# A transformer block for eight sequences: an earlier start of batch 0, one tile earlier for batch 3, and q's rows stored ahead of k's reading

## The chip, the cores and the metric

The kernel runs on one core of a Trainium2 chip. The metric is the device time of one execution in microseconds, the median of several runs. A profile is one such execution, taken with the hardware profiler.

## The reference, cut to what matters

The input is eight sequences of 512 tokens with 256 features. Each goes through three steps, and each step adds to the sequence:

```python
x = x + 0.5 * ffn(layernorm(x))        # ffn: fft, times a sparse 256x256 complex matrix, real part of ifft, + bias
x = x + attention(layernorm(x))        # q, k, v from the left 128 features; 16 heads of 8; softmax; Wo; + bo
x = x + 0.5 * ffn(layernorm(x))
```

The ffn is linear, so the kernel folds it at its start into one real matrix of 256x256, `half_ffn`, that already holds the factor 0.5. The mean and the variance of the layernorm are taken beside the product: x1 = (product of the raw rows) * rstd + x + half of the bias.

## The kernel before, in words

Five engines run side by side, each with an instruction list of its own that is carried out strictly in its written order: TensorE (`pe`, the matmuls), ScalarE (`act`, above all the exponentials), VectorE (`dve`, everything that leaves PSUM), GpSimd (`pool`, the reciprocal roots and the additions of biases) and SyncE (`sp`, the transfers). Semaphores are the only link: an engine that waits holds all that stands behind it in its list.

The work for one batch is cut into 16 quads of four heads by 128 keys. For a quad TensorE makes the scores (`score_products`, L799), ScalarE the exponentials (L669, two instructions of 128x1024), and TensorE multiplies them with the values (`value_quad`, L828) into the bank `ot`. The outer loop (`it`, L908 and on) goes over the batches, and the inner one over 16 slots `s`. In a slot TensorE issues the scores of the next quad, then the jobs of the slot, then the products of this quad with the values.

The jobs are the rest of the work: `F1_t` (first ffn of tile t), `LT`/`KT`/`QT`/`V` (normed left half transposed, keys, queries, values), `N` (norms for the guard), `WO_t` (output product) and `F2_t` (second ffn). Which job runs in which slot for which batch is written in tables at the file's head: `BEGIN` for iteration 0, `FIRST` for iteration 1, `STEADY`, `LATE` and `END` for the others. An entry `("F1_1", 2, LEFT)` in iteration 1 works for batch 3. All jobs share the bank `misc`; a job waits on TensorE until VectorE has evacuated all jobs of earlier slots.

Two helpers on VectorE matter here. `left_half(b)` (L957) subtracts the mean and multiplies with the reciprocal root; it waits for `rstd_done[1]`, which GpSimd raises in `rstd_of(1, ...)` (L548 and L550). `turn_left(b)` (L966) transposes the result into `left_blocks`; SyncE stores that to `left_scr` and loads it back as `leftT`, from which `KT_0` is made in slot 14. The calls in the loop over slots are

```python
if s == (8 if it else 10):
    left_half(it + 2, range(0, 2))
if s == (9 if it else 10):
    left_half(it + 2, range(2, T))
    if it:
        turn_left(it + 2)
```

GpSimd's list for iteration `it` is `end_of(it - 1)` (L563, L553 for x_out), `rstd_of(2, it)`, which waits for the moments of x2 that VectorE makes at the end of slot 5 (L946), `begin_x2(it)` (two additions of 128x512, L563 and L553), and only then `rstd_of(1, it + 3)`.

The keys and queries of a batch are spread over the partitions by way of memory: `k_out` stores `kp` to `k_scr` (L393), `k_in` loads it back as `KS` in two transfers (L400), `q_out` and `q_in` do the same with `qp`, `q_scr` and `QS` (L396, L404). SyncE issues all of them.

A guard (`guard`, L833) decides for each batch whether the scores are so large that an exact branch has to compute the attention. TensorE loads the flag from memory into a register and branches. With these inputs the branch isn't taken.

Before the loops lies an opening (`PROLOGUE`): the folding of the ffn, F1 of batches 0 and 1, LT, KT, QT, V and N of batch 0, and the first two score quads.

## Time and profile before

| what | value |
|---|---|
| median of three runs | 315.89 us (313.49 to 320.12) |
| the profiled execution's own time | 312.38 us |
| its span | 310.5 us |
| TensorE busy in the span | 294.8 us (95%) |
| ScalarE busy | 257.6 us (83%) |
| VectorE busy | 190.5 us (61%) |
| GpSimd busy | 98.3 us (32%) |
| TensorE's granted clock | full in every slice |

The span goes from the first to the last instruction; 1.9 us of the execution's own time lie outside of it. Times in the rows below count from the start of the span. PE is the matmuls of TensorE and PEld its weight loads, DVE is VectorE, ACT is ScalarE, POOL is GpSimd, SPq is what SyncE issues. In a row of the timeline the first number is the start, the second the time until the end of the last instruction of the row, then the engine, the line, the operation, what it writes and reads, the number of instructions, and in brackets how long the engine had been idle before it and what ended that.

### The profile page before, as it was taken

Reading aid. Unit: us, or ns where it says so; the run is one execution under the profiler, and the core shown is the slowest. Engines: PE = TensorE matmul, PEld = TensorE weight load, DVE = VectorE, ACT = ScalarE, POOL = GpSimd, SP = SyncE. Lnnn points to the kernel's source line nnn. Section 1 sums busy time; section 2 is a strip of 40 time slices with the busy share of each in tenths; the row PEclk is TensorE's granted clock in tenths of the full one; section 3 lists DMA queues with packets and bytes.
Section 4 is the critical chain, followed back from the end, with each engine's and each line's share of the span. In section 5 each row is a group of like instructions: output and inputs, shape, how many; then the busy total and the mean of one; then the engine's idle time right before and its main releaser. Section 6 shows DMA issues by size and latency. Waiting matters only on the chain.

```text
span 310.5 us, 8810 instructions
## 1 busy us (share of the span) xinstructions
PE 294.8 (95%) x3440; PEld 112.5 (36%) x3443; DVE 190.5 (61%) x552; ACT 257.6 (83%) x285; POOL 98.3 (32%) x113
## 2 busy tenths in 40 slices
PE   8887999899998999999999999999999999998996
PEld 5633333233332333333333333334333333322333
DVE  1688546747775678657776678567755643370255
ACT  2117998898997889998998989998999999999921
POOL 6562531223604053223604251313600340034005
PEclk9999999999999999999999999999999999999999
DMA  7935615573462762665453663554372464112102
GB/s 192 337 137 192 218 65 153 195 270 133 139 217 83 245 208 103 208 204 217 155 192 129 231 205 112 198 172 143 131 238 104 138 205 170 38 68 70 37 34 70
DMA packets 25891, 49.33 MB, mean 159 GB/s; under 512 B 2032, under 2 KB 14192, under 8 KB 24048
## 3 DMA queue, kind: packets, MB, share of 16 engines
q1 hardware_dynamic: 25152, 48.26, 46.0%
q10 hardware_dynamic: 688, 0.40, 0.8%
q8 instruction: 32, 0.52, 0.7%
q14 instruction: 19, 0.16, 0.2%
HBM read 31.08 MB, written 17.56 MB: 157 GB/s over the span
## 4 chain that ended last, share of the span: by engine, by line
PE 75%; DMA 9%; DVE 5%; ACT 5%; issue 3%; POOL 3%; SPq 0%; ACTq 0%; POOLq 0%
PE ot L828 28%; PE misc L719 26%; PE scores L799 15%; ACT probs L669 5%; DMA leftT<-left_scr 4%; DMA q_scr<-qp 2%; PE scores L719 2%; DMA QS<-q_scr 2%; DMA left_scr<-left_blocks 1%; POOL x L553 1%; PE scores L686 1%; PE scores L693 1%; DVE left_blocks L966 1%; DVE lh L957 1%; POOL rstd L550 1%
## 5 line engine op out<-in xcount | busy, mean ns | idle before, releaser
L669 ACT ACTIVATE probs<-scores 128x1024 f32<-128x1024 f32 x256 | 243.8, 1028 | 20.6 <-PE scores L799 20.3
L828 PE MATMUL ot<-probs,VS 128*32 128x512 f32 x1024 | 133.9, 594 | 2.9 <-ACT probs L669 2.3
L799 PE MATMUL scores<-QS,KS 32*128 32x512 f32 x512 | 64.7, 495 | 3.0 <-DMA QS<-q_scr 1.3
L799 PEld LDWEIGHTS scores<-QS,KS 32*128 32x128 f32 x512 | 24.5, 181 | 109.8 <-ACT probs L669 101.0
L828 PEld LDWEIGHTS ot<-probs,VS 128*32 128x32 f32 x1024 | 30.6, 109 | 25.8 <-ACT probs L669 5.0
L563 POOL TENSOR_TENSOR x_out<-x,half_bias 128x512 f32<-128x512 f32 x7 | 9.0, 1292 | 88.8 <-DVE x L1012 88.8
L548 POOL TENSOR_SCALAR veps<-mv 128x4 f32<-128x4 f32 (+1 forms) x25 | 6.1, 242 | 95.9 <-DVE mv L946 95.9
L1017 DVE SCALAR_TENSOR_TENSOR x_out<-misc,rstd,x_out 128x256 f32<-128x256 f32 x28 | 13.5, 484 | 33.7 <-PE misc L719 30.2
L719 PE MATMUL misc<-half_ffn,xT 128*32 128x256 f32 x448 | 32.1, 386 | 0.0
L719 PE MATMUL misc<-half_ffn,xT_in 128*32 128x256 f32 x400 | 27.1, 385 | 1.4 <-DVE half_ffn L1193 1.3
L550 POOL TENSOR_TENSOR rstd<-veps,power 128x4 f32<-128x4 f32 (+1 forms) x25 | 25.3, 1013 | 2.1
L939 DVE BATCH_NORM_STATS2 stats<-x 128x6 f32<-128x256 f32 x64 | 23.2, 411 | 0.0
L1012 DVE TENSOR_TENSOR x<-misc,x 128x256 f32<-128x256 f32 x30 | 11.3, 419 | 16.7 <-PE misc L719 16.7
L993 DVE SCALAR_TENSOR_TENSOR x<-misc,rstd,x_in 128x256 f32<-128x256 f32 x24 | 11.6, 484 | 14.8 <-PE misc L719 14.8
L553 POOL TENSOR_TENSOR x_out<-x,half_bias 128x512 f32<-128x512 f32 x9 | 11.5, 1285 | 19.7 <-DVE x L1012 19.7
L1056 DVE STREAM_TRANSPOSE ot_t<-ot 128x512 f32<-128x512 f32 x16 | 11.5, 716 | 8.8 <-PE ot L828 8.8
L719 PE MATMUL misc<-wo_sb,otn 128*32 128x256 f32 x240 | 16.1, 385 | 0.6 <-DVE otn L1070 0.6
L972 DVE STREAM_TRANSPOSE x_blocks<-x 128x512 f32<-128x512 f32 x14 | 16.3, 1165 | 0.5
L719 PEld LDWEIGHTS misc<-half_ffn,xT 128*32 128x32 f32 x448 | 10.9, 108 | 11.7 <-issue 5.6
L719 PEld LDWEIGHTS misc<-half_ffn,xT_in 128*32 128x32 f32 x400 | 10.4, 109 | 11.8 <-issue 5.1
L983 DVE CAST kp<-misc 128x256 fp32r<-128x256 f32 x14 | 5.9, 424 | 13.8 <-PE misc L719 12.5
L939 DVE BATCH_NORM_STATS2 stats<-x_in 128x6 f32<-128x256 f32 x32 | 11.6, 410 | 0.0
(125 smaller groups left out, 260.0 us busy)
## 6 DMA issues: line engine op xcount, KB each, us to landing
KS<-k_scr SPq DMA_DIRECT2D x14, 512.0 KB, 4.9
QS<-q_scr SPq DMA_DIRECT2D x14, 512.0 KB, 4.6
x_in<-x SPq DMA_DIRECT2D x8, 512.0 KB, 5.1
xT_in<-x_t SPq DMA_DIRECT2D x8, 512.0 KB, 6.4
k_scr<-kp SPq DMA_DIRECT2D x8, 512.0 KB, 3.0
q_scr<-qp SPq DMA_DIRECT2D x8, 512.0 KB, 4.4
x_scr<-x_blocks SPq DMA_DIRECT2D x7, 512.0 KB, 2.9
xT<-x_scr SPq DMA_DIRECT2D x7, 512.0 KB, 4.7
```

Of the source, the lines that this page charges most:

```text
L550: nc.gpsimd.tensor_tensor(to[:, tiles], veps[k][:, tiles], power[:, tiles], ALU.pow).then_inc(rstd_done[k], 1)
L553: nc.gpsimd.tensor_tensor(dst[:, tiles, :], src[:, tiles, :], row[:, :].unsqueeze(1).to_broadcast([P, tiles.stop - tiles.start, E]), ALU.a ...
L669: nc.scalar.activation(probs[u % PRING][:, :, :], scores[u % SRING][:, :, :], ACT.Exp, scale=SCORE_SCALE).then_inc(exp_done, 1)
L719: last = mm(dst[COL * j:COL * (j + 1), :], weights(j), rhs, start=c == 0, stop=c == len(terms) - 1)
L799: last = mm(scores[(u + j // 2) % SRING][:, j % 2, :], KS[b % 2][rows, slot, kt * P:(kt + 1) * P].bitcast(F32R), QS[b % 2][rows, slot, :]. ...
L828: last = mm(ot[COL * j:COL * (j + 1), :], VS[b % 2][:, kt, h, :], probs[(u + j // 2) % PRING][:, j % 2, :], start=s % 8 == 0, stop=s % 8 == 7)
L939: ins = nc.vector.bn_stats(stats[k][:, t, :], src[:, t, :])
L972: last = nc.vector.transpose(x2_blocks[:, :, 2 * i:2 * i + 2, :], x2[:, 2 * i:2 * i + 2, :].rearrange("p t (f k) -> p k t f", k=E // 32))
L993: return nc.vector.scalar_tensor_tensor(x1[b % 3][:, i, :], tile, rstd[0][b % 2][:, i:i + 1], biased[:, i, :], ALU.mult, ALU.add)
L1012: nc.vector.tensor_tensor(x2[:, i, :], tile, x2[:, i, :], ALU.add).then_inc(evacuated, 1)
L1017: nc.vector.scalar_tensor_tensor(x_out[:, i, :], tile, rstd[2][0][:, i:i + 1], x_out[:, i, :], ALU.mult, ALU.add).then_inc(evacuated, 1)
L1056: nc.vector.transpose(ot_t[:, :, :].rearrange("p c r -> p (c r)"), ot[:, :]).then_inc(ot_taken, 1)
```

## The change

- **Opening.** `half_bias` is made between ScalarE's four copies and not behind them. GpSimd adds it to tiles 0 and 1 of batch 0 ahead of its first reciprocal root. VectorE makes the statistics of x1 of batch 0 for tiles 0 and 1 as soon as they are there, GpSimd takes their roots apart from those of tiles 2 and 3, and two of the four statistics of batch 1's input are made first. The evacuation of F1_3 of batch 1 is moved behind those of KT and QT.
- **Values of batch 0's first quad.** `value_products(0, 0)` is issued ahead of the guard's branch, and once more inside of the branch, which isn't taken.
- **Iteration 1.** F1_1, F1_2 and F1_3 of batch 3 move from slots 4, 5 and 6 to slots 1, 4 and 5; slot 6 is empty. `left_half` of batch 3 moves from slots 8 and 9 to 7 and 8, with `turn_left` in slot 8.
- **Transfers.** `q_out(1)` stands ahead of `k_in(1)`.

On TensorE, around the first guard. Before (the register load of L835 follows the second score quad at once):

```order
L799 MATMUL scores<-QS,KS 128x512 x4
L788 MATMUL misc<-kp,pick 128x512 x2
L788 MATMUL ot<-qp,pick 128x512 x2
L799 MATMUL scores<-QS,KS 128x512 x4
L835 TENSOR_LOAD safe
L835 ISA x2
L836 COMPARE_AND_BRANCH
```

and with the change, where `ot<-probs,VS` is the first value product:

```order
L810 MATMUL scores<-QS,KS 128x512 x4
L799 MATMUL misc<-kp,pick 128x512 x2
L799 MATMUL ot<-qp,pick 128x512 x2
L810 MATMUL scores<-QS,KS 128x512 x4
L844 MATMUL ot<-probs,VS 32x512 x4
L851 TENSOR_LOAD safe
L851 ISA x2
L852 COMPARE_AND_BRANCH
```

The four value matmuls now stand ahead of the load of the flag.

On VectorE, slots 5 to 9 of iteration 1 (`x_0<-misc` is x1 of batch 3, `x` the x2 of batch 0, `lh` the normed left half, `VS` the values). Before:

```order
L946 BN_AGGR mv<-stats 128x2 x4
L993 SCALAR_TENSOR_TENSOR x_0<-misc,rstd_1,x_in 128x256
L939 BN_STATS stats<-x_0 128x6 x2
L946 BN_AGGR mv<-stats 128x2 x4
L983 CAST qp<-misc 128x256
L985 TENSOR_TENSOR qp<-misc,qp 128x256
L1056 STREAM_TRANSPOSE ot_t<-ot 128x512
L983 CAST qp<-misc 128x256
L985 TENSOR_TENSOR qp<-misc,qp 128x256
L957 TENSOR_SCALAR lh<-x_0,mv,rstd_0 128x128 x2
L1030 COPY VS<-misc 128x16x8 x4
L957 TENSOR_SCALAR lh<-x_0,mv,rstd_0 128x128 x2
```

and with the change:

```order
L966 BN_AGGR mv<-stats 128x2 x4
L959 BN_STATS stats<-x 128x6 x2
L966 BN_AGGR mv<-stats 128x2 x4
L1004 CAST qp<-misc 128x256
L1006 TENSOR_TENSOR qp<-misc,qp 128x256
L1077 STREAM_TRANSPOSE ot_t<-ot 128x512
L978 TENSOR_SCALAR lh<-x_0,mv,rstd_0 128x128 x2
L1004 CAST qp<-misc 128x256
L1006 TENSOR_TENSOR qp<-misc,qp 128x256
L978 TENSOR_SCALAR lh<-x_0,mv,rstd_0 128x128 x2
L987 STREAM_TRANSPOSE left_blocks<-lh 128x512
L1051 COPY VS<-misc 128x16x8 x4
```

The first half of `lh` stands ahead of the second evacuation of q, and `left_blocks` ahead of the values; the moments of x2 are the second of the two groups of `mv` and no longer the first.

On SyncE, the rows of batch 1. Before:

```order
L393 DMA k_scr<-kp 128x2x512
L400 DMA KS<-k_scr 64x1x2048 x2
L396 DMA q_scr<-qp 128x2x512
L404 DMA QS<-q_scr 64x1x2048 x2
L393 DMA k_scr<-kp 128x2x512
```

and with the change:

```order
L399 DMA k_scr<-kp 128x2x512
L402 DMA q_scr<-qp 128x2x512
L406 DMA KS<-k_scr 64x1x2048 x2
L410 DMA QS<-q_scr 64x1x2048 x2
L399 DMA k_scr<-kp 128x2x512
```

The store of q is issued ahead of the two loads of k.

```diff
@@ -74,7 +74,8 @@
           12: [("F2_1a", -1, LEFT), ("F2_1", -1, LEFT)], 13: [("F2_2a", -1, LEFT), ("F2_2", -1, LEFT)],
           14: [("KT_0", 2, RIGHT)], 15: [("KT_1", 2, RIGHT)]}
 
-FIRST = {**STEADY, 0: [("F1_0a", 2, LEFT), ("F1_0", 2, LEFT)], 1: []}
+FIRST = {**STEADY, 0: [("F1_0a", 2, LEFT), ("F1_0", 2, LEFT)], 1: [("F1_1a", 2, LEFT), ("F1_1", 2, LEFT)],
+         4: [("F1_2a", 2, LEFT), ("F1_2", 2, LEFT)], 5: [("F1_3a", 2, LEFT), ("F1_3", 2, LEFT)], 6: []}
 
 BEGIN = {3: [("LT", 1, LEFT)], 4: [("KT_0", 1, RIGHT), ("F1_0a", 2, LEFT)], 5: [("F1_0", 2, LEFT), ("QT_0", 1, RIGHT)],
          6: [("KT_1", 1, RIGHT), ("F1_1a", 2, LEFT)], 7: [("F1_1", 2, LEFT), ("QT_1", 1, RIGHT)],
@@ -103,7 +104,7 @@
     if it == PROLOGUE:
 
         ahead = [(f"F1_{t}", 2) for t in range(T)]
-        jobs = [(f"F1_{t}", 1) for t in range(T)] + [("LT", 1)] + ahead + [("KT", 1), ("QT", 1), ("N", 1)]
+        jobs = [(f"F1_{t}", 1) for t in range(T)] + [("LT", 1)] + ahead[:-1] + [("KT", 1), ("QT", 1), ahead[-1], ("N", 1)]
         return {s: [(name, d, LEFT)] for s, (name, d) in enumerate(jobs)}
     if it == EPILOGUE:
 
@@ -319,6 +320,11 @@
         mv_done = [sem(f"mv_done{i}") for i in range(3)]
         veps_done = [sem(f"veps_done{i}") for i in range(3)]
         rstd_done = [sem(f"rstd_done{i}") for i in range(3)]
+        ahead_biased = sem("ahead_biased")
+        first_stats = sem("first_stats")
+        first_mv = sem("first_mv")
+        first_veps = sem("first_veps")
+        first_rstd = sem("first_rstd")
         normed = sem("normed")
         ahead_ready = sem("ahead_ready")
         left_turned = sem("left_turned")
@@ -500,8 +506,8 @@
 
             load_x(3)
             k_out(1)
+            q_out(1)
             k_in(1)
-            q_out(1)
             q_in(1)
             for it in range(1, B):
                 if it + 1 < B:
@@ -581,15 +587,20 @@
                 rstd_of(0, b + 1)
                 add_rows(x_in[b % 2], x_in[b % 2], half_bias, xb_done)
 
-            rstd_of(0, 1)
             pool.wait_ge(bias_set, 1)
             pool.wait_ge(x_loaded[0], 16)
             add_row(x1[0], x_in[0], half_bias, early_biased, slice(0, 1))
             add_row(x1[0], x_in[0], half_bias, early_biased, slice(1, 2))
+            rstd_of(0, 1)
             add_row(x1[0], x_in[0], half_bias, xb_done, slice(2, T))
             pool.wait_ge(x_loaded[1], 16)
-            add_rows(x1[1], x_in[1], half_bias, xb_done)
-            rstd_of(1, 1)
+            add_row(x1[1], x_in[1], half_bias, ahead_biased, slice(0, 2))
+            pool.wait_ge(first_mv, 1)
+            nc.gpsimd.tensor_scalar(veps[1][:, 0:2], mv[1][:, 0:2, 1], EPS, None, ALU.add).then_inc(first_veps, 1)
+            pool.wait_ge(first_veps, 1)
+            nc.gpsimd.tensor_tensor(rstd[1][0][:, 0:2], veps[1][:, 0:2], power[:, 0:2], ALU.pow).then_inc(first_rstd, 1)
+            rstd_of(1, 1, slice(2, T))
+            add_row(x1[1], x_in[1], half_bias, xb_done, slice(2, T))
             rstd_of(0, 2)
             square(kp, sq_k, kp_step, 0)
             square(qp, sq_q, qp_step, 0)
@@ -629,12 +640,12 @@
             for piece, bank, copy in ((1, scores[0][:, 0], even[0]), (3, scores[1][:, 0], even[1])):
                 act.wait_ge(ffn_mm, piece)
                 nc.scalar.copy(copy[:, :, :], half_bank(bank)).then_inc(ffn_copied, 1)
+            act.wait_ge(bias_loaded, 16)
+            nc.scalar.mul(half_bias[:, :], bias_raw[:, :], 0.5).then_inc(bias_set, 1)
             for piece, bank, copy in ((5, scores[0][:, 0], even[2]), (6, scores[0][:, 1], odd)):
                 act.wait_ge(ffn_mm, piece)
                 nc.scalar.mul(copy[:, :, :], half_bank(bank), 0.5 / E).then_inc(ffn_copied, 1)
 
-            act.wait_ge(bias_loaded, 16)
-            nc.scalar.mul(half_bias[:, :], bias_raw[:, :], 0.5).then_inc(bias_set, 1)
             act.wait_ge(pick_loaded, 16)
             nc.scalar.copy(pick[:, :, :, :, :].rearrange("p n s i r -> p (n s i r)").bitcast(F32R),
                            pick_raw[:, :, :, :, :].rearrange("p n s i r -> p (n s i r)")).then_inc(pick_set, 1)
@@ -824,10 +835,15 @@
                 if s % 8 == 0:
                     wait(pe, ot_taken, 2 * b + g)
                 pe.wait_ge(exp_done, u + 2)
+                value_products(b, s).then_inc(quad_done, 1)
+
+            def value_products(b, s):
+                _, _, kt, heads = quad_units(s)
+                u = PAIRS * b + 2 * s
                 for j, h in enumerate(heads):
                     last = mm(ot[COL * j:COL * (j + 1), :], VS[b % 2][:, kt, h, :],
                               probs[(u + j // 2) % PRING][:, j % 2, :], start=s % 8 == 0, stop=s % 8 == 7)
-                last.then_inc(quad_done, 1)
+                return last
 
             def guard(b, taken):
 
@@ -864,6 +880,8 @@
                         pe.wait_ge(exact_taken, done + 1)
                         mm(misc[:, 0:E], attnT[:, :], wo_sb[:, :], start=True, stop=True).then_inc(exact_ready, 1)
                     pe.wait_ge(guarded, b + 1)
+                    if b == 0:
+                        value_products(0, 0)
                 with pe.Else():
                     pe.sem_inc(exact_ready, EXACT_MM)
 
@@ -901,6 +919,7 @@
             pe.wait_ge(evacuated, evac_count("N", 0))
             first_rows(3)
             score_quad(0, 1)
+            value_quad(0, 0)
             guard(0, evac_count("N", 0))
             pe.wait_ge(late_loaded, 32)
 
@@ -915,7 +934,8 @@
                     if it == 0 and 0 < s < 3:
                         keep_awake(1, misc[:, :])
                     run_jobs(it, s)
-                    value_quad(it, s)
+                    if it or s:
+                        value_quad(it, s)
                     if s == guard_slot(it) and it + 1 < B:
                         guard(it + 1, count_of_slots_to(it, s))
 
@@ -952,7 +972,8 @@
                     norm_stats(0, x_in[b % 2], t, t == T - 1)
 
             def left_half(b, tiles=range(T)):
-                dve.wait_ge(rstd_done[1], b + 1)
+                if b or tiles[-1] == T - 1:
+                    dve.wait_ge(rstd_done[1], b + 1)
                 for t in tiles:
                     last = nc.vector.tensor_scalar(lh[:, t, :], x1[b % 3][:, t, 0:HD], mv[1][:, t, 0:1],
                                                    rstd[1][0][:, t:t + 1], ALU.subtract, ALU.mult)
@@ -1202,20 +1223,41 @@
             norm0_stats(0)
             norm_moments(0, 1)
             fold(half_ffn, even[2], odd[:, :, :], ALU.subtract, ALU.add, 6, 4)
-            for s in range(T):
-                run_jobs(PROLOGUE, s)
-            norm0_stats(1)
-            left_half(0)
+            dve.wait_ge(mv_done[0], 1)
+            norm0_stats(1, range(0, 2))
+
+            def first_x1(t):
+                dve.wait_ge(evacuated, evac_count(f"F1_{t}", 0))
+                return nc.vector.bn_stats(stats[1][:, t, :], x1[0][:, t, :])
+
+            evacuate("F1_0", 0)
+            evacuate("F1_1", 0)
+            first_x1(0)
+            evacuate("F1_2", 0)
+            first_x1(1).then_inc(first_stats, 1)
+            dve.wait_ge(first_stats, 1)
+            for t in range(2):
+                last = nc.vector.bn_aggr(mv[1][:, t, :], stats[1][:, t, :])
+            last.then_inc(first_mv, 1)
+            evacuate("F1_3", 0)
+            first_x1(2)
+            first_x1(3).then_inc(stats_done[1], 1)
+            norm_moments(1, 1, range(2, T))
+            dve.wait_ge(first_rstd, 1)
+            left_half(0, range(0, 2))
+            norm0_stats(1, range(2, T))
+            left_half(0, range(2, T))
             norm_moments(0, 2)
 
-            run_jobs(PROLOGUE, T)
-            for t in range(T):
+            evacuate("LT", 0)
+            for t in range(T - 1):
                 evacuate(f"F1_{t}", 1)
-            run_jobs(PROLOGUE, 2 * T + 1)
-            run_jobs(PROLOGUE, 2 * T + 2)
+            evacuate("KT", 0)
+            evacuate("QT", 0)
+            evacuate(f"F1_{T - 1}", 1)
             dve.wait_ge(row_ready, 1)
             nc.vector.tensor_copy(KS[0][:, 0, :].bitcast(F32R), row_banks[0]).then_inc(first_k_set, 1)
-            run_jobs(PROLOGUE, 2 * T + 3)
+            evacuate("N", 0)
             for n, rows in ((2, KS[0][:, 1, :]), (3, QS[0][:, 1, :])):
                 dve.wait_ge(row_ready, n + 1)
                 nc.vector.tensor_copy(rows.bitcast(F32R), row_banks[n]).then_inc(second_set, 1)
@@ -1248,9 +1290,9 @@
                                 norm_stats(2, x2, t, t == T - 1)
                             norm_moments(2, it)
                     if it + 2 < B:
-                        if s == (8 if it else 10):
+                        if s == (10 if not it else 7 if it == 1 else 8):
                             left_half(it + 2, range(0, 2))
-                        if s == (9 if it else 10):
+                        if s == (10 if not it else 8 if it == 1 else 9):
                             left_half(it + 2, range(2, T))
                             if it:
                                 turn_left(it + 2)
```

## Rows read from the trace of the kernel before

**Rows 1.** The page: the chain that ended last, by engine.

```profile
PE 75%; DMA 9%; DVE 5%; ACT 5%; issue 3%; POOL 3%; SPq 0%; ACTq 0%; POOLq 0%
```

**Rows 2.** The waits of PE over the span: us in total, times, longest.

```profile
PE misc L719 <- DMA leftT<-left_scr: 1.8, 2, 1.5
```

**Rows 3.** Timeline of the opening, 12 to 21 us.

```profile
12.64 2.66 POOL L553 TENSOR_TENSOR x<-x_in,half_bias 128x256 f32<-128x256 f32 x3
...
13.47 0.48 DVE L993 SCALAR_TENSOR_TENSOR x<-misc,rstd,x 128x256 f32<-128x256 f32 x1 [1.70 <-POOL x L553]
...
19.17 1.12 DVE L957 TENSOR_SCALAR lh<-x,mv,rstd 128x128 f32<-128x128 f32 x4 [0.20 <-POOL rstd L550]
...
20.40 0.42 PEld L753 LDWEIGHTS misc<-ident,lh 128*128 128x128 f32 x4 [1.42 <-issue]
```

**Rows 4.** The instructions of GpSimd that write rstd, over the whole span.

```profile
L550 POOL TENSOR_TENSOR rstd<-veps,power x25: 715/1038/1052, 11.6 to 306.3; 128x4 f32<-128x4 f32 x23, 128x2 f32<-128x2 f32 x2
```

**Rows 5.** Timeline around the first guard, 29 to 32 us.

```profile
29.95 0.19 PEld L828 LDWEIGHTS ot<-probs,VS 128*32 128x32 f32 x8 [1.31 <-issue]
...
30.98 0.19 PEld L799 LDWEIGHTS scores<-QS,KS 32*128 32x128 f32 x4 [0.84 <-ACT probs L669]
...
31.54 7.51 ACT L669 ACTIVATE probs<-scores 128x1024 f32<-128x1024 f32 x8 [0.39 <-PE scores L799]
```

**Rows 6.** Timeline, the rows of k and q of batch 1, 46 to 63 us.

```profile
46.03 0.42 DVE L985 TENSOR_TENSOR qp<-misc,qp 128x256 fp32r<-128x256 f32 x1
...
48.80 1.16 SPq L400 DMA_DIRECT2D KS<-k_scr  x2
...
50.00 0.59 SPq L396 DMA_DIRECT2D q_scr<-qp  x1
...
62.44 3.77 ACT L669 ACTIVATE probs<-scores 128x1024 f32<-128x1024 f32 x4 [1.34 <-PE scores L799]
```

**Rows 7.** Timeline of iteration 1, score quads of slots 1 to 3 on PE.

```profile
65.82 0.51 PE L799 MATMUL scores<-QS,KS 32*128 32x512 f32 x4
...
67.45 0.51 PE L799 MATMUL scores<-QS,KS 32*128 32x512 f32 x4
...
69.75 0.50 PE L799 MATMUL scores<-QS,KS 32*128 32x512 f32 x4
```

**Rows 8.** Timeline of iteration 1, 77 to 87 us, DVE, POOL and PE.

```profile
77.41 0.38 DVE L946 BATCH_NORM_AGGREGATE mv<-stats 128x2 f32<-128x6 f32 x4
...
78.19 1.04 POOL L550 TENSOR_TENSOR rstd<-veps,power 128x4 f32<-128x4 f32 x1
...
79.20 1.28 POOL L563 TENSOR_TENSOR x<-x,bo_sb 128x512 f32<-128x512 f32 x1
...
80.92 0.72 DVE L1056 STREAM_TRANSPOSE ot_t<-ot 128x512 f32<-128x512 f32 x1
...
82.01 1.04 POOL L550 TENSOR_TENSOR rstd<-veps,power 128x4 f32<-128x4 f32 x1
...
83.08 0.61 DVE L957 TENSOR_SCALAR lh<-x,mv,rstd 128x128 f32<-128x128 f32 x2 [0.28 <-POOL rstd L550]
83.11 0.81 PEld L719 LDWEIGHTS misc<-wv_sb,leftT 128*32 128x32 f32 x32 [0.24 <-DVE qp L985]
...
85.69 1.21 DVE L966 STREAM_TRANSPOSE left_blocks<-lh 128x512 f32<-128x512 f32 x1
```

**Rows 9.** Timeline of iteration 1, what SyncE issues, and PE behind it.

```profile
87.30 1.26 SPq L404 DMA_DIRECT2D QS<-q_scr  x2
...
95.33 0.19 PEld L719 LDWEIGHTS misc<-leftT,wk_sb 128*32 128x32 f32 x8 [1.76 <-issue]
```

**Rows 10.** Landing times of the transfers of q_scr and QS, 0 to 100 us.

```profile
DMA to landing us min/median/max: 3.6/4.4/6.4
```

**Rows 11.** Timeline, the same dummy matmul at the start and later.

```profile
1.18 3.56 PE L693 MATMUL scores<-waking 128*128 128x512 bf16 x9 [1.18 <-DVE waking L1196]
...
20.89 0.59 PE L693 MATMUL scores<-waking 128*128 128x512 bf16 x2
```

## Prediction

> **What bounds the kernel now.** I read the chain that ended last, then the waits of each engine, then the timeline wherever the two show a stall. The chain is 75% TensorE and 9% transfers [rows 1]. In the loop a slot with a full job costs 2.30 us from one score quad to the next, and a slot without one costs 1.63 us behind it [rows 7]: TensorE is the limit in slots with jobs, ScalarE trails closely. An edit is worth something only where TensorE or ScalarE stands still. There are three such places ahead of 100 us: the opening (the first exponentials start at 27.38 us, and nothing of batch 0 can run before), 1.34 us of ScalarE when iteration 1 waits for the rows of q [rows 6], and TensorE's wait of about 1.5 us for leftT, its longest of the whole loop [rows 2, 9]. The change touches all three. The reader should also see a fourth place that isn't a stall yet: GpSimd's list in iteration 1, which ends just as VectorE asks for it [rows 8].
>
> **The opening.** VectorE's first x1 waits 1.70 us for GpSimd's addition [rows 3], because GpSimd makes the reciprocal root first and adds behind it from 12.64. With the additions moved ahead (they need half_bias, now made before ScalarE's last two copies), the first x1 can start once the root is there at about 12.7 and the product at 12.9: half a microsecond sooner. More comes from taking the roots in two halves. Before, the normed left half starts at 19.17 and LT on TensorE at 20.40 [rows 3]. Now the first half's root is ready at about 16.9 (moments at 15.8, 0.24 for veps, then a two-column root at 0.72, the shortest in [rows 4]), the second's at about 18.3. VectorE ends the left half near 19.1 to 19.3. LT then starts at about 19.5, since TensorE has its F1 products and two dummy matmuls until then. That is 0.9 us, and the chain behind it (copy of leftT, KT, split, QT, split, rows, first scores) moves along; moving F1_3 of batch 1 behind the splits takes 0.4 us from the wait for kp, but the copy of q's row by ScalarE is what the first scores wait for, and that gains 0.9 to 1.1. I take 1.0 us, with 0.5 (the additions alone) and 1.4 (F1_3 counting in full) as ends.
>
> **The values ahead of the guard.** Before: the guard's load and branch hold TensorE's weights for 1.31 us behind the second score quad, the values come at 29.95, the third score quad at 30.98, and ScalarE has stood idle for 0.39 us when it is done [rows 5]. So guard and values lie one behind the other and 2.5 us pass from 28.45 to 30.98. Now the values wait for the second exponential (0.9 us after the second score quad starts), and the same 1.45 us of guard follow their issue: 0.9 + 0.1 + 1.45 = 2.45. The order changes, the sum doesn't. I take 0; the best case is ScalarE's idle 0.39 us, the worst 0.3 lost where the flag's load is held up by the matmuls' issue. The copy inside of the branch isn't executed.
>
> **q's rows ahead of k's reading.** q was ready at 46.45 but its store went out at 50.00, because SyncE first waited until k was stored and issued KS at 48.80 [rows 6]. It took the longest of all, 6.4 us, beside the load of KS; the shortest took 3.6 [rows 10]. Now it goes out at once, lands by about 50 to 52, and QS follows at the latest by 58, ahead of the 60.5 at which TensorE could use it. ScalarE's gap of 1.34 us [rows 6] goes whole: it is busy until 61.1. Bounds: 1.34 and 0 (below). What waits next is nothing: with the gap closed ScalarE is the limit there. GpSimd's half of x for F1_0 of batch 3 ends at 63.75 in the old time and is then due within 0.1 us.
>
> **Iteration 1: where it costs.** Moving the F1 jobs keeps the sum of slots: one slot of 2.30 and one of 1.63 change places [rows 7], so slots 2 to 5 lie 0.65 us later and slot 7 where it was. But look at what VectorE does in slot 5. It now holds F1_3, the last one, with the x1 statistics of two tiles and the moments (0.41 + 0.74 + 0.38) before the statistics and moments of x2. The moments of x2, at 77.41 to 77.79 before [rows 8], then end near 79.2: 0.65 for the slot and 0.75 for one more statistic and the other moments. GpSimd waits for exactly these. Its list behind them is fixed: veps and root (1.04 at 78.19), two additions for x2 from 79.20, then veps and the root for batch 3, 82.01 to 83.05 [rows 8]. All of it moves by 1.4 us: that root comes at about 84.45.
>
> VectorE used to ask for it at 82.80, behind the second evacuation of q, and waited 0.28 us [rows 8]. Now `left_half` stands in slot 7 ahead of that evacuation: VectorE arrives when its transposition of `ot` is done, at 81.64, and stands until 84.45, 2.8 us. Behind it in its list are the evacuation of QT_1 and everything after; TensorE's V job of slot 9 waits for that evacuation, and V started at 83.11, with no slack [rows 8]. With 0.61 for the two instructions of lh and 0.88 for cast and subtraction, QT_1 is evacuated at about 85.95 and V starts at 86.0: 2.9 us later. The values of that slot stand behind V, so ScalarE runs dry too. Then lh's second half and the transposition (1.21) stand ahead of the copy of V: another 0.4 us for N. I take 3.3 us; the ends are 1.2 (only the old order of GpSimd's list: the root at 83.05, with no later moments) and 3.6. No later slot gives it back: slots with jobs run at TensorE's own pace.
>
> **leftT.** Part of that returns. In the old time `left_blocks` ends at 86.9, QS for batch 2 is issued at 87.30 behind it, and leftT is used at 95.33, 8.0 us after QS's issue, 1.5 us late [rows 8, 9]. Now q's store goes at 86.0, `left_blocks` ends at 87.7, q's store lands at 86.0 + 3.6 = 89.6 by the shortest of [rows 10], QS is issued then, and leftT lands at 96.9 to 97.5. TensorE would want it at 93.8 + 3.3 = 97.1. So the wait shrinks from 1.5 to between 0 and 0.4: I take 1.3 back, bounds 0 and 1.5.
>
> **Sum.** -1.0 + 0 - 1.3 + 3.3 - 1.3 = -0.3 us. Against the profiled execution's own 312.38 (span and 1.9 around it) that is 312.1. The three timed runs have a median of 315.89 and reach from 313.49 to 320.12, so the profiled one is quicker than any of them. The middle of the four readings is 314.7; less 0.3, and leaning a little to the median, I forecast 315.0. In these runs no difference below about 2%, 6.3 us, can be told from none.
>
> **Rivals.** *The hold costs nothing.* If VectorE's wait in slot 7 were short or hidden, the rest stands: -1.0 - 1.3 - 1.3 = -3.6, 311.4 on the same footing. For it: such a wait at the same place was 0.28 us before. Against it: the list of GpSimd runs without a gap from 78.19 to 83.05 [rows 8], so the root can't come before the question at 81.64. 15%.
>
> *The transfers don't follow* (the other side). The hold stays at 3.3, but q's store lands no sooner because it now shares the engines with k's, QS of batch 1 stays behind KS, and leftT stays 1.5 us late: -1.0 + 3.3 = +2.3, 317.3. It decides from the point where QS of batch 1 lands after 60.5 in the old time. For it: k's store was issued at 43.8 and KS could only be issued at 48.80, with little else under way; landings are erratic. Against it: q would have to take more than twice its median of 4.4. 15%.
>
> *The clock.* TensorE has no wait of more than 1.5 us in the loop and a granted clock that never falls [rows 2]. The hold is nearly twice as long, so a fall isn't excluded by any row. What it would cost shows at the start, where nine dummy matmuls take 3.56 us against 0.59 for two later [rows 11]: (0.40 - 0.21) x 9 = 1.6 to 1.8 us. So -0.3 + 1.7 = +1.4, 316.4. 8%. The Trainium skill ("TensorE: Matmul & The Clock Gate", the part on the HAM clock gate) says that the engine goes back to its half rate after idling for a while; in this trace every stall left the clock full, and no row has one as long as this.
>
> *The new order of values and guard does nothing at all* is in the forecast already.
>
> **Chances and range.** Forecast 62%, hold hidden 15%, transfers 15%, clock 8%. All cases lie within 2% of 315.9, so the spread of the measurement decides: the runs before differ by 2%. Range 310.5 to 319.0: it takes in 311.4 and 317.3 and the spread of a median of three. Faster by over 2%: 0.08. Slower by over 2%: 0.05. Within: 0.87.
>
> **What would show it.** In the profile after: first exponential at 26.3 to 26.5 us (opening); third score quad still 2.5 us behind the second (values); ScalarE's gap at the start of iteration 1 gone; in slot 7 of iteration 1 an idle time of VectorE of about 2.8 us before lh, ended by GpSimd's rstd, and one of TensorE of about 2.9 before V, ended by VectorE's qp; leftT's wait under 0.5. No such wait on VectorE, or x2's moments as early as before, would make the main step wrong. If the opening moves by less than 0.5 us, the first step is.

## The result, and the profile after

The changed kernel takes 315.51 us (median of 22 runs, 313.06 to 320.01); the kernel before, run beside it, 312.81 us (22 runs, 309.73 to 320.12). The ratio is 1.0085, with a 95% interval from 1.0061 to 1.0109: about 2.7 us slower (1.9 to 3.4), where the prediction had 0.3 us faster. The ratio leaves out executions more than 1.5% above the fastest of their kernel, three of the 22 here. By the 2% that the chances go by, that is "within 2%", and the time lies in the range, close to the 315.0 that was forecast. That closeness is luck: the forecast stood on the 315.89 of three runs of the kernel before, whose median over 22 runs is 312.81. With this many runs the sign can be told, and it is the other one. The profiled execution of the changed kernel took 314.41 us with a span of 312.5, against 312.38 and 310.5 before.

The place the prediction worried about is the place that costs. First the timeline of iteration 1 of the changed kernel, VectorE (DVE) and GpSimd (POOL) (start us, duration us, engine, line, operation; in brackets the idle time before it and what ended it), beside [rows 8]:

```profile
77.97 0.38 DVE L966 BATCH_NORM_AGGREGATE mv<-stats 128x2 f32<-128x6 f32 x4
...
78.75 1.04 POOL L556 TENSOR_TENSOR rstd<-veps,power 128x4 f32<-128x4 f32 x1
...
79.70 0.42 DVE L1006 TENSOR_TENSOR qp<-misc,qp 128x256 fp32r<-128x256 f32 x1
79.76 1.29 POOL L569 TENSOR_TENSOR x<-x,bo_sb 128x512 f32<-128x512 f32 x1
80.14 0.72 DVE L1077 STREAM_TRANSPOSE ot_t<-ot 128x512 f32<-128x512 f32 x1
...
81.00 1.28 POOL L559 TENSOR_TENSOR x<-x,bo_sb 128x512 f32<-128x512 f32 x1
...
82.56 1.04 POOL L556 TENSOR_TENSOR rstd<-veps,power 128x4 f32<-128x4 f32 x1
...
83.63 0.60 DVE L978 TENSOR_SCALAR lh<-x,mv,rstd 128x128 f32<-128x128 f32 x2 [2.77 <-POOL rstd L556]
```

VectorE stands 2.77 us for GpSimd's second root; the prediction had 2.8. The four POOL rows show why: root, two additions and root follow each other, with nothing between them but the short veps (0.23 us) of the second root, and all of it hangs on the moments at 77.97. Next TensorE (PE) in the same stretch:

```profile
81.93 0.51 PE L810 MATMUL scores<-QS,KS 32*128 32x512 f32 x4
85.08 1.93 PE L730 MATMUL misc<-wv_sb,leftT 128*32 128x128 f32 x32 [2.64 <-DVE qp L1006]
86.78 1.60 PE L844 MATMUL ot<-probs,VS 128*32 128x512 f32 x8
88.32 0.51 PE L810 MATMUL scores<-QS,KS 32*128 32x512 f32 x4
```

V waits 2.64 us for VectorE's evacuation of q (forecast: 2.9 us later). The reader should then look at the durations: V takes 1.93 and the values 1.60, where the same instructions take 1.08 and 1.04 at their ordinary pace. From V's start to the next score quad pass 3.24 us, not 1.86 (85.64 to 87.50 in *Busy through the hold* below). The busy shares and the granted clock (PEclk) by microsecond tell why (columns: stretch, its length, busy shares of PE, PEld, DVE, ACT, POOL with instruction counts, granted clock, DMA share, GB/s):

```profile
83.00:84.00 1.00, 0.00 (x0) 0.00 (x0) 0.37 (x2) 0.00 (x0) 0.59 (x1) 1.00 0.00 0
84.00:85.00 1.00, 0.00 (x0) 0.00 (x0) 0.97 (x4) 0.40 (x1) 0.00 (x0) 0.76 0.00 0
85.00:86.00 1.00, 0.92 (x20) 0.86 (x24) 0.97 (x4) 1.00 (x2) 0.00 (x0) 0.50 0.04 14
86.00:87.00 1.00, 1.00 (x24) 0.92 (x20) 0.70 (x1) 1.00 (x2) 0.00 (x0) 0.50 1.01 389
87.00:88.00 1.00, 1.00 (x10) 0.00 (x0) 0.89 (x4) 0.06 (x1) 0.00 (x0) 0.54 0.76 293
88.00:89.00 1.00, 1.00 (x16) 0.43 (x16) 0.00 (x0) 0.12 (x1) 0.00 (x0) 1.00 0.28 98
```

TensorE idles, its clock falls from 2.4 to 1.2 GHz (1.00 to 0.50) while it idles, and it comes back to work at half pace until 88. This is the rival that had 8%. In 11 of the 22 runs the mean clock of the whole run is 0.995 or less (median 316.2 us), in the other 11 it is 0.999 or 1.000 (median 314.4). A mean does not tell where the clock fell: the kernel before, which has no such wait, has a mean of 0.995 or less in 15 of the 128 runs of the experiments whose clock is listed. So up to half of the executions pay for a fall at the hold, more likely some 40%, and the 1.7 us between the two medians need not all be this fall.

The remaining parts, in the waits of TensorE over the span (us in total, times, longest; against [rows 2]):

```profile
PE misc L730 <- DVE qp L1006: 2.6, 1, 2.6
...
PE misc L730 <- DMA leftT<-left_scr: 0.6, 1, 0.6
```

The wait of 1.5 us for leftT is gone from iteration 1; the 0.6 stands in iteration 3 (at 166.36). So is the gap of q: ScalarE (ACT) has a row of twelve activations with no idle time through the start of iteration 1, and q's store goes out at once behind its evacuation, on SyncE (SPq), against [rows 6]:

```profile
46.83 0.38 SPq L402 DMA_DIRECT2D q_scr<-qp  x1
49.11 1.16 SPq L406 DMA_DIRECT2D KS<-k_scr  x2
50.36 1.20 SPq L410 DMA_DIRECT2D QS<-q_scr  x2
...
53.95 11.38 ACT L680 ACTIVATE probs<-scores 128x1024 f32<-128x1024 f32 x12 [0.37 <-PE scores L810]
```

In the opening, the first exponentials start 15.88 us after the folding's last subtraction begins (11.80 to 27.68), where it was 16.37 (11.01 to 27.38): 0.5 us gained. That they start later on the axis of the profile comes from ahead of the folding's end: its last subtraction begins 0.8 us later in this execution, where TensorE's first folding matmul waits for the load of `wre_sb` (PEld at 4.57, 0.28 us) and the second group of them starts at 6.37, before at 5.48. At the guard, the third score quad starts 2.57 us behind the second (28.76 to 31.33), before 2.53. And one pair of rows, VectorE and GpSimd, 17 to 21 us, shows something that the prediction had not in it:

```profile
17.81 0.58 DVE L978 TENSOR_SCALAR lh<-x,mv,rstd 128x128 f32<-128x128 f32 x2
...
18.97 1.27 POOL L559 TENSOR_TENSOR x<-x_in,half_bias 128x512 f32<-128x512 f32 x1
19.04 1.55 DVE L978 TENSOR_SCALAR lh<-x,mv,rstd 128x128 f32<-128x128 f32 x2
```

The same two instructions take 0.58 us the first time and 1.55 the second, beside an addition by GpSimd. The durations of the four single instructions say it more sharply: the least is 318 ns, the median 340 ns, and one took 1293 ns.

### The profile page after: what moved, and what is told of

Its sections match the earlier page's. It is cut to its first block, busy times and chain, and to the rows that moved or that the text cites. A ratio compares the mean times of both kernels' runs of the same rounds, so it can differ in the third digit from the quotient of the medians.

```text
span 312.5 us, 8813 instructions
## 1 busy us (share of the span) xinstructions
PE 297.2 (95%) x3440; PEld 113.8 (36%) x3443; DVE 191.7 (61%) x552; ACT 257.6 (82%) x285; POOL 98.8 (32%) x115
## 4 chain that ended last, share of the span: by engine, by line
PE 79%; DVE 7%; ACT 4%; issue 4%; DMA 3%; POOL 1%; SPq 0%; ACTq 0%; POOLq 0%; DVEq 0%
PE ot L844 29%; PE misc L730 27%; PE scores L810 15%; ACT probs L680 4%; PE scores L730 2%; DMA leftT<-left_scr 2%; DMA q_scr<-qp 2%; PE scores L697 1%; PE scores L704 1%; DVE stats L959 1%; PE ot L730 1%; DVE lh L978 1%; PE misc L764 1%; DVE qp L1006 1%; DVE qp L1004 1%
## 5 line engine op out<-in xcount | busy, mean ns | idle before, releaser
L959 DVE BATCH_NORM_STATS2 stats<-x 128x6 f32<-128x256 f32 x60 | 21.7, 412 | 0.0
L978 DVE TENSOR_SCALAR lh<-x,mv,rstd 128x128 f32<-128x128 f32 x32 | 10.4, 371 | 5.3 <-POOL rstd L556 5.3
```

The lines of the kernel that those rows point to most:

```text
L959: ins = nc.vector.bn_stats(stats[k][:, t, :], src[:, t, :])
L978: last = nc.vector.tensor_scalar(lh[:, t, :], x1[b % 3][:, t, 0:HD], mv[1][:, t, 0:1], rstd[1][0][:, t:t + 1], ALU.subtract, ALU.mult)
```

## The experiments

Several theories are named in the expectations. H: the loss is VectorE's hold for GpSimd's root and what stands behind it. C: part of it is TensorE's clock. P: VectorE's left half and GpSimd's addition shut each other out. T, the rival of H: the new table of jobs itself costs (in *Roots first*, T stands for the early place in VectorE's list). O, the rival in the first four: part of the loss lies outside of iteration 1, or the gains there don't exist. Ratios are to the kernel before, run on the same chip in the same rounds, with 95% intervals.

**One part alone.** First the change cut in pieces.

*Opening only.* The whole of the change in GpSimd's, ScalarE's and VectorE's lists of the opening, of which the core is

```diff
+            add_row(x1[1], x_in[1], half_bias, ahead_biased, slice(0, 2))
...
+            left_half(0, range(0, 2))
+            norm0_stats(1, range(2, T))
+            left_half(0, range(2, T))
```

with values, iteration 1 and q as before:

> Only the opening of the change. Theory H (the loss is the hold in iteration 1): the first exponential starts 0.5 us sooner after half_ffn is done than before, and the time falls by 0.5 us. Theory O (part of the loss is outside iteration 1): 0 to 1.5 us slower, although the first exponentials aren't later. In both, the second pair of lh takes 1.5 us beside GpSimd's addition, against 0.6 for the first pair.

Measured: 1.0017 (0.9981 to 1.0053), 0.5 us from folding to first exponential in the trace, the slow pair of lh there too (1.55). The half microsecond doesn't reach the time measurably.

*Values only:*

```diff
+            value_quad(0, 0)
             guard(0, evac_count("N", 0))
```

> The kernel before with batch 0's first values ahead of the guard's branch and again inside it, and nothing else of the change. The prediction says that only the order changes: third score quad 2.5 us behind the second, as before, ratio 0.998 to 1.002. Rival (the values ahead of the branch hold up the flag's load, or save the wait): the distance is over 2.8 or under 2.2 us and the ratio leaves 1.000 by 0.001.

Measured: 1.0013 (0.9973 to 1.0052), third score quad 2.55 us behind the second (29.32 to 31.87). A zero, as forecast.

*q's store only:*

```diff
             k_out(1)
+            q_out(1)
             k_in(1)
-            q_out(1)
```

> Only q's store of batch 1 ahead of k's reading. Theory H: ScalarE's gap of 1.34 us at the start of iteration 1 goes, and the time falls by 1.3 us. Theory O: the gap goes, but the time falls by less than 0.5 us, because a later wait takes its place.

Measured: 0.996 (0.9924 to 0.9996), no wait for QS. It is the one part that gains, and the only kernel here whose interval lies below the one before, if barely: among fourteen kernels, one such interval is weak evidence.

*Iteration 1 only*, the kernel before with

```diff
-FIRST = {**STEADY, ..., 1: []}
+FIRST = {**STEADY, ..., 1: [("F1_1a", 2, LEFT), ("F1_1", 2, LEFT)],
+         4: [("F1_2a", 2, LEFT), ("F1_2", 2, LEFT)], 5: [("F1_3a", 2, LEFT), ("F1_3", 2, LEFT)], 6: []}
...
-                        if s == (8 if it else 10):
+                        if s == (10 if not it else 7 if it == 1 else 8):
...
-                        if s == (9 if it else 10):
+                        if s == (10 if not it else 8 if it == 1 else 9):
```

> Only the iteration-1 part (the table of slots and left_half one slot earlier). Theory H: VectorE waits 2.8 us before lh, TensorE 2.6 us before V, and its clock drops to half behind that in some runs; 2.6 us slower with the drop (4.1 for the hold and the slow matmuls, less 1.5 for leftT), 1.2 us without it. Theory O: at most 1 us slower.

Measured: 1.0086 (1.0047 to 1.0126), the whole loss of the change. Its profile has the waits to the hundredth (2.77 on VectorE, 2.64 on TensorE), but V takes 1.08 us: in that execution the clock stayed full there, while the mean was 0.995 or less in 6 of its 12 runs. The profiled execution was a long one all the same, 318.77 us, with 5.7 us of waits for leftT in iterations 2 to 5; only its iteration 1 and its wait for QS are used below.

*All but iteration 1:* the changed kernel with these lines turned back, each + and - exchanged.

> The change without its iteration-1 part. Theory H: 1.8 us faster than before (0.5 and 1.3), no fall of the clock. Theory O: no faster than before, with TensorE's wait for leftT still at 1.5 us or longer.

Measured: 0.9995 (0.996 to 1.003). Without iteration 1's part the change costs nothing, but it gains nothing that shows either: the 1.8 us that H expected lie outside of the interval (1.2 us at most). On this side O was right. The longest wait for leftT is 1.47 us, as O said, but it stands in iteration 3 (at 162.80); in iteration 1 there is none.

**What in iteration 1.** The table or the early place, the wait or the clock?

*Left half late*, the table kept:

```diff
-                        if s == (10 if not it else 7 if it == 1 else 8):
+                        if s == (8 if it else 10):
...
-                        if s == (10 if not it else 8 if it == 1 else 9):
+                        if s == (9 if it else 10):
```

> The changed kernel with the left half of batch 3 back at its old places in iteration 1 (slots 8 and 9, behind the evacuation of QT_1); the new table of F1 jobs stays. Theory H (the loss is VectorE's hold for GpSimd's root, and what stands behind it in VectorE's list): TensorE's wait for qp ahead of V (2.64 us) falls under 0.5, no fall of the clock at 84 to 88 us, and the time comes to 0.997 to 1.002 of the kernel before. Rival T (the table itself costs: TensorE's slots and the later moments of x2): the ratio stays at 1.005 to 1.009.

Measured: 0.9988 (0.995 to 1.0026). VectorE still waits 1.62 us for the root, but behind the evacuation of QT_1, and TensorE's wait for qp is gone. Against the 0.9995 without any of iteration 1's part, T falls: the table without the early place costs nothing that shows in the time. In the profile iteration 1 is 34.20 us long, some 0.6 more than with the old table; 0.4 of that is N on TensorE, which waits for VectorE's copy of V.

*Early left half, old table:*

```diff
-FIRST = {**STEADY, ..., 1: [("F1_1a", 2, LEFT), ("F1_1", 2, LEFT)],
-         4: [("F1_2a", 2, LEFT), ("F1_2", 2, LEFT)], 5: [("F1_3a", 2, LEFT), ("F1_3", 2, LEFT)], 6: []}
+FIRST = {**STEADY, ..., 1: []}
```

> The changed kernel with the old table of F1 jobs in iteration 1; the left half of batch 3 stays early, in slots 7 and 8. Of the hold of 2.77 us on VectorE the prediction puts 1.4 on the table (the later moments of x2) and the rest on the early place. If that is right, VectorE's wait for the root is 1.2 to 1.5 us here, TensorE's for qp 1.1 to 1.5, iteration 1 takes 35.0 to 35.6 us, the clock falls in none or few executions, and the ratio to the kernel before is 1.002 to 1.005. Rival (GpSimd's list doesn't start with the moments of x2, the whole hold is the early place): both waits stay over 2.3 us and the ratio is 1.006 or more.

Measured: the waits are 1.43 on VectorE and 1.33 on TensorE, as expected, and iteration 1 takes 35.04 us from first score quad to first score quad. The ratio is 1.0002 (0.9965 to 1.0038), below the 1.002 to 1.005 that was expected: a wait of 1.3 us of TensorE does not show in a time with an interval of 1.1 us to either side. Of the hold, then, 1.3 us is the moments of x2 that the table makes late, and 1.4 the early place. The mean clock is 0.995 or less in 2 of the 12 runs here, and in 6 of 12 and 11 of 22 where both come together.

*Roots first.* The moments of batch 3's left rows are ready at 76.9, ahead of those of x2, and GpSimd could use them at once:

```diff
                 end_of(it - 1)
+                if it == 1:
+                    rstd_of(1, it + 3)
                 rstd_of(2, it)
                 begin_x2(it)
-                if it + 2 < B:
+                if it + 2 < B and it != 1:
                     rstd_of(1, it + 3)
```

> The changed kernel, with GpSimd in iteration 1 making the root of batch 3's left rows ahead of the root for x2 and of the two additions, where the moments of batch 3 (ready at 76.9 us) allow it; VectorE's and TensorE's lists stay. Theory H: the wait of 2.77 us on VectorE and the one of 2.64 on TensorE go to 0.3 or less, no fall of the clock, and since the wait for leftT stays short the time is 2.5 to 4 us below that of the changed kernel: a ratio to the kernel before of 0.996 to 1.001. Rival T (the early left half costs by its place in VectorE's list, not by the wait for the root): V still comes over 1 us late and the ratio stays above 1.004.

Measured: 1.0037 (1.0006 to 1.0068), short of H's expectation and just below its rival's. The wait for the root is gone, but V still waits 1.05 us, as the rival said. The timeline of VectorE and GpSimd says for what:

```profile
79.82 1.28 POOL L569 TENSOR_TENSOR x<-x,bo_sb 128x512 f32<-128x512 f32 x1
...
80.57 1.86 DVE L980 TENSOR_SCALAR lh<-x,mv,rstd 128x128 f32<-128x128 f32 x2
...
81.06 1.28 POOL L559 TENSOR_TENSOR x<-x,bo_sb 128x512 f32<-128x512 f32 x1
82.35 0.41 DVE L1006 CAST qp<-misc 128x256 fp32r<-128x256 f32 x1
```

The pair of lh takes 1.86 us and ends at 82.43, with the second addition (82.34). It is the opening's finding again.

*Additions behind V*, on top of it:

```diff
                 rstd_of(2, it)
+                if it == 1:
+                    pool.wait_ge(evacuated, evac_count("V_1", it + 1))
                 begin_x2(it)
```

> The kernel with the roots first in iteration 1 (e7), and now GpSimd's two additions for x2 wait for the evacuation of V_1, so that none runs beside the first pair of the early left half (which took 1.86 us there, between additions from 79.82 to 82.34). Theory P (VectorE's left half and GpSimd's addition shut each other out): that pair takes 0.6 us, TensorE's wait for qp of 1.05 us goes under 0.2, and the ratio to the kernel before falls from 1.0037 to 0.999 to 1.002. Rival: the pair is slow for another reason, keeps its 1.8 us, and the ratio stays at 1.003 to 1.005.

Measured: 0.9984 (0.9948 to 1.0021). VectorE and GpSimd:

```profile
80.21 0.56 DVE L982 TENSOR_SCALAR lh<-x,mv,rstd 128x128 f32<-128x128 f32 x2
80.69 0.41 DVE L1008 CAST qp<-misc 128x256 fp32r<-128x256 f32 x1
...
84.15 1.28 POOL L569 TENSOR_TENSOR x<-x,bo_sb 128x512 f32<-128x512 f32 x1 [4.67 <-DVE VS L1055]
```

and TensorE, where V follows its score quad without a wait:

```profile
81.35 0.51 PE L814 MATMUL scores<-QS,KS 32*128 32x512 f32 x4
81.79 1.08 PE L734 MATMUL misc<-wv_sb,leftT 128*32 128x128 f32 x32
```

With table and early place as in the changed kernel, and the two waits taken away, the loss is gone: about 1% below the changed kernel. So T falls in its second form too, and H and P both stand.

*Busy through the hold:*

```diff
+                    if it == 1 and s == 9:
+                        for _ in range(8):
+                            mm(ot[:, :], waking[:, 0:P], waking[:, :], start=False, stop=False)
                     run_jobs(it, s)
```

> The changed kernel, with eight matmuls of zeros (128x512 each, some 1.7 us at the full clock, added into the bank of the values, which they leave as it is) ahead of V in slot 9 of iteration 1, while VectorE is held up. Theory C (part of the loss is TensorE's clock, which falls in about half of the executions after the wait of 2.6 us): the granted clock stays at 1.00 there, V with its values takes about 1.9 us instead of 3.2, and the median falls by 0.7 to 1.5 us, a ratio to the kernel before of 1.004 to 1.006. Rival: the clock is a bystander, the ratio stays at 1.008 or rises.

Measured: 1.0044 (1.0011 to 1.0077). The hold of 2.77 us on VectorE is unchanged, but TensorE:

```profile
83.15 1.67 PE L938 MATMUL ot<-waking 128*128 128x512 bf16 x7 [0.16 <-issue]
85.64 1.08 PE L730 MATMUL misc<-wv_sb,leftT 128*32 128x128 f32 x32 [0.81 <-DVE qp L1009]
86.53 1.04 PE L844 MATMUL ot<-probs,VS 128*32 128x512 f32 x8
```

The granted clock is 1.00 in every microsecond from 82 to 89. V and values are at full pace (1.86 us to the next score quad), and the mean clock is under 0.996 in 1 of 12 runs. Nothing else was changed, so C stands as to the clock: useless work in the wait keeps it up. What it buys is less certain: 1.0085 less 1.0044 is 1.3 us of the 2.7, but the two intervals overlap, and together they allow from nothing to 2.6 us. By the profiles, iteration 1 is 36.45 us long here and 37.57 in the changed kernel.

**The other engine's addition.** *Addition later*, in the opening:

```diff
             rstd_of(1, 1, slice(2, T))
-            add_row(x1[1], x_in[1], half_bias, xb_done, slice(2, T))
             rstd_of(0, 2)
+            add_row(x1[1], x_in[1], half_bias, xb_done, slice(2, T))
```

> The changed kernel, with GpSimd's addition for tiles 2 and 3 of batch 1 moved behind the root for batch 1, so that it no longer runs beside the second pair of VectorE's left half. Theory P (the two engines hold each other up: one instruction of lh took 1.29 us there instead of 0.33, as long as the addition): the second pair of lh takes 0.6 to 0.7 us instead of 1.55, and LT on TensorE starts about 0.9 us sooner after the folding. Rival (VectorE's instruction waits for the second half of the root or for statistics, not for the addition's traffic): the pair still takes over 1.3 us. In the time: 0 to 0.9 us below the changed kernel, a ratio to the kernel before of 1.005 to 1.009.

Measured: 1.0083 (1.0037 to 1.013). The second pair of lh:

```profile
19.41 0.60 DVE L978 TENSOR_SCALAR lh<-x,mv,rstd 128x128 f32<-128x128 f32 x2
```

0.60 us, so P is right here too, and the opening comes to the gain that the prediction gave it: 0.9 us from folding to first exponential against the kernel before (16.37 to 15.49). LT starts 8.30 us after the folding's last step begins (12.17 to 20.47), not 8.93 (11.80 to 20.73): 0.6, since TensorE's own products now end last. Against the changed kernel, 0.4 are left by the first exponential, because the F1 evacuations of batch 1 wait 1.29 us for the addition that was put off, and kp stands behind them. In the time nothing shows.

**Mended versions, and a control.**

*All together* (left half late, roots first, additions behind V, the opening's addition later):

> The changed kernel with all that the runs so far suggest: left half of batch 3 late (slots 8 and 9), GpSimd's roots first in iteration 1, its additions there behind V_1, and in the opening the addition for tiles 2 and 3 of batch 1 behind the root. If losses and gains add up as the traces show (e6 at 0.9988, VectorE's wait of 1.62 us for the root gone with the 0.37 us of TensorE's N and 0.41 of ScalarE behind it, 0.4 us more in the opening), the ratio to the kernel before is 0.995 to 0.998. Rival (these gains are hidden or given back to the transfers, as the opening's was): 0.998 to 1.001, no different from e6.

Measured: 1.0013 (0.998 to 1.0047), the rival. Its timeline shows that the additions, released by V's evacuation, now fall onto the late second pair of lh:

```profile
83.35 1.56 DVE L982 TENSOR_SCALAR lh<-x,mv,rstd 128x128 f32<-128x128 f32 x2
83.51 1.32 POOL L569 TENSOR_TENSOR x<-x,bo_sb 128x512 f32<-128x512 f32 x1 [4.42 <-DVE VS L1055]
```

and N's maxima come late for it (a wait of 0.71 us on TensorE for norms). Iteration 1 is 34.59 us long: that is where its gain went.

*The same without the opening:* the kernel before with q's store, the new table, and the roots and additions of iteration 1 as above; opening, values and left half as before.

> The kernel before with q's rows stored ahead of k's reading, the new table of F1 jobs in iteration 1, the left half late as before, GpSimd's roots first and its additions behind V_1 there; opening and guard as before. Against e12 it tells what the opening is worth: if its 0.5 to 0.9 us reach the end, this kernel is 0.002 to 0.003 slower than e12; if they are given back, both are the same. Against e3 (0.996: q's store alone) it tells whether the table gains anything once VectorE isn't held: if so 0.992 to 0.995, if not 0.996 or above.

Measured: 1.0054 (1.0018 to 1.009). Against *All together* that is 0.4% slower, where 0.2 to 0.3% was expected if the opening's gain reaches the end; the two intervals overlap. Against q's store alone the table gains nothing, rather it loses. It has the same collision as *All together* (a pair of 1.56 at 84.97, 0.7 for norms), and in its profile four waits for leftT, 3.6 us together, where the other has 0.7. Whether those waits belong to this kernel or to this execution stays open, and with it what the opening is worth: *Opening only* and *All but iteration 1* show no gain from it.

*The kernel before, again:*

> The kernel before, unchanged, once more, for a second profile and as a measure of what this comparison calls different. The prediction gave back 1.3 us because TensorE waits 1.48 us for leftT in iteration 1 of the profile of before. If that wait belongs to the kernel, it stands in this profile too, iteration 1 takes 34.9 us from first score quad to first score quad, and the profiles of the runs with the old table (33.4 to 33.6 without such a wait) are the odd ones. Rival: the wait is one execution's, this profile shows under 0.5 us and an iteration 1 of 33.4 to 33.8. The ratio is 1.000 within 0.004 by either.

Measured: 0.9985 (0.995 to 1.0021) against itself, and the profile sides with the rival: iteration 1 takes 33.39 us, TensorE doesn't wait for leftT in it, and ScalarE runs through the start of iteration 1 with no gap at all:

```profile
54.63 11.21 ACT L669 ACTIVATE probs<-scores 128x1024 f32<-128x1024 f32 x12 [0.36 <-PE scores L799]
...
162.80 0.64 PE L719 MATMUL misc<-leftT,wk_sb 128*32 128x256 f32 x8 [0.60 <-DMA leftT<-left_scr]
```

The only wait for leftT that is left stands at 162.80, in iteration 3. Both waits that the prediction took as gains are absent from a second execution of the same program.

Put side by side, from the profiles (us; iteration 1 is from its first score quad to that of iteration 2, and a 0 in the waits stands for one too short to be listed, under 0.2):

| kernel | wait for QS | wait for leftT, it. 1 | wait for leftT, all | wait for qp, it. 1 | iteration 1 |
|---|---|---|---|---|---|
| before | 1.3 | 1.5 | 1.8 | 0 | 34.91 |
| before again | 0 | 0 | 0.6 | 0 | 33.39 |
| values only | 0.3 | 0 | 0.9 | 0 | 33.37 |
| opening only | 1.1 | 0 | 3.6 | 0 | 33.58 |
| q's store only | 0 | 0 | 2.6 | 0 | 33.59 |
| all but iteration 1 | 0 | 0 | 3.5 | 0 | 33.41 |
| old table, early left half | 0 | 0 | 3.4 | 1.3 | 35.04 |
| iteration 1 only | 0.3 | 0 | 5.7 | 2.6 | 36.39 |
| changed kernel (clock falls) | 0 | 0 | 0.6 | 2.6 | 37.57 |
| addition later (clock falls) | 0 | 0 | 0.9 | 2.7 | 37.83 |
| busy through the hold | 0 | 0 | 1.0 | 0.8 + dummies | 36.45 |
| left half late | 0 | 0 | 1.4 | 0 | 34.20 |
| roots first | 0 | 0 | 2.9 | 1.1 | 34.82 |
| additions behind V | 0 | 0 | 2.1 | 0 | 33.56 |
| all together | 0 | 0.3 | 0.7 | 0 | 34.59 |
| the same without the opening | 0 | 0.5 | 3.6 | 0 | 34.82 |

The old iteration 1 takes 33.4 to 33.6 us, the held one 36.4, and 37.6 to 37.8 where the clock falls. The fourth column is the one to learn from: the change leaves the instructions of the later iterations as they are, and yet TensorE's waits for leftT there come to anything from 0.3 us (before) to 5.7 (iteration 1 only). The two profiles of one program, before and before again, differ by 1.2 us in this column.

## Why the prediction was wrong

**The hold: right, in place, cause and size.** 2.77 of 2.8 us on VectorE, 2.64 of 2.9 on TensorE, ended by the instructions named. It costs 36.4 less 33.5 = 2.9 us of an iteration without the clock; the forecast was 3.3, of which 0.4 for a late N. The slot with N takes 2.18 us in *Iteration 1 only* (87.34 to 89.52) and 1.95 before (84.98 to 86.93), so 0.2 of the 0.4 is there.

**leftT: this is the first step that failed.** The step was "the wait shrinks from 1.5 to between 0 and 0.4: I take 1.3 back". The wait did shrink to 0, but there was nothing to shrink: of seven profiles with the old table (the first six rows of the table and the old table with the early left half) one has the wait, and it is the one I had read. Its mean over them is 0.2 us. The prediction treated a landing time of one execution as a property of the kernel, though it noted itself that landings reach from 3.6 to 6.4 us [rows 10].

**q's store: the same error, smaller.** Forecast -1.3, the whole gap of one profile. Over the five profiles with SyncE's old order the wait is 1.3, 1.1, 0.3, 0.3 and 0, 0.6 on average; the part alone measures 0.4% of 312.5, 1.2 us, with an interval from 0.1 to 2.4. The mechanism (store at once, QS behind KS) is as described.

**The clock: the second step that failed.** The forecast put it at nothing and gave the rival 8%, since no row had so long a wait. The mean clock is low in 11 of 22 runs, against 15 of 128 of the kernel before. The price, by [rows 11] 1.6 to 1.8 us, is 1.2 to 1.4 in iteration 1 of the two profiles that have the fall (37.57 and 37.83 less 36.4), and 1.7 between the medians of the runs with and without it. That makes 0.5 us on the average over all runs by the lower figures (1.2 us in 40%) and 0.9 by the higher (1.7 in half). The price was about right; the chance was not. The prediction's sentence on the Trainium skill ("TensorE: Matmul & The Clock Gate", the part on the HAM clock gate) pointed the right way: idling did drop the engine to its half rate. The rival was put at +1.4 overall, half of what was measured.

**The opening: half of it.** Forecast -1.0 with 0.5 as an end; 0.5 in the traces, and nothing measurable in the time (1.0017 for the opening only). What took the other half is the second pair of lh, 1.55 us beside GpSimd's addition, which I had counted at the 0.6 us that it takes alone. The diff shows the addition right behind the root that releases this pair.

**The values: right**, 0.

**The sum over.** From the profiles: -0.5 (opening) + 0 - 0.6 (q) + 2.9 (hold) + 0.5 to 0.9 (clock) - 0.2 (leftT) = +2.1 to +2.5 us, against 2.7 measured (1.9 to 3.4). From the runs: -0.2 for all but iteration 1 (0.9995) and +2.7 for iteration 1 only (1.0086) make +2.5. The forecast of -0.3 came out by setting 3.6 us of gains against 3.3 of loss; of the gains 1.3 are in the profiles, and in the time -0.2, with an interval from -1.2 to +0.9. The loss was certain, because it hangs on the order of instructions; most of the gains were waits for transfers. One slip rests in the times of the rivals: 311.4, 317.3 and 316.4 take their changes from 315.0, which holds the -0.3 already, so each is 0.3 too low. No conclusion hangs on it.

## What to carry to other kernels

A wait that an order of instructions makes is there in every execution; a wait for a transfer, read from one profile, may be that execution's own: before it is counted as a gain, see it in a second profile, or weight it. Before an instruction is moved ahead in an engine's list, follow what it waits for through the other engine's list, and see whether that list can be turned as well: here the roots first and the additions behind V together cured what the early left half broke. And a new stall of TensorE, longer than any in the trace at hand (2.64 us against 1.5 here), is to be priced with a fall of the clock behind it.
